# Loading the expert, down and output weights and the bias from SP's queue behind the first inputs, in a fused attention and expert layer

## The reference

```python
def attn(x, w_qkv, w_out):                       # 16 heads of 8
    q, k, v = split(x @ w_qkv)
    a = softmax(q @ k.T / sqrt(128))
    return (a @ v) @ w_out

def ffn(x, Wr, Wg, Wu, Wd, Sg, Su, Sd, bias):    # 8 experts, 2 taken, 1 shared
    top_v, top_i = top_k(x @ Wr + bias, 2)
    rw = zeros.at[top_i].set(softmax(top_v))
    h = silu(x @ Wg) * (x @ Wu)
    return sum_e(rw[e] * (h[e] @ Wd[e])) + silu(x @ Sg) * (x @ Su) @ Sd

x = x + layernorm(attn(layernorm(x)))
x = x + layernorm(ffn(layernorm(x)))
```

## Time and profile before

| | |
|---|---|
| median of 3 runs | 380.06 us (378.44 to 380.81) |
| span of the profiled execution | 378.7 us |
| PE busy | 359.4 us (95%) |
| DVE busy | 310.7 us (82%) |
| ACT busy | 267.4 us (71%) |
| POOL busy | 200.8 us (53%) |
| DMA, moved | 45.65 MB |

### The profile page before, as it was taken

The page is one execution under the profiler, slowest core; times in us unless marked ns, Lnnn a source line. Parts: engine busy times, 40 slices in busy tenths (PEclk is TensorE's granted clock), DMA queues, the critical chain, the costliest instruction groups (busy, mean ns, idle before and its releaser), DMA issues.

```text
span 378.7 us, 10110 instructions
## 1 busy us (share of the span) xinstructions
PE 359.4 (95%) x3342; PEld 231.8 (61%) x3342; DVE 310.7 (82%) x788; ACT 267.4 (71%) x511; POOL 200.8 (53%) x518
## 2 busy tenths in 40 slices
PE   7898799999999999999999999999999999999992
PEld 7866556455465557575657565665665566677872
DVE  8476579989899998989998889999998896767461
ACT  4563368788977877887878877786868876964522
POOL 5723121615556374848472835674744655858644
PEclk9999899999999999999999999999999999999998
DMA  2139766847534728557616937544773042222201
GB/s 76 44 105 150 180 123 131 183 140 153 148 105 137 181 54 205 142 144 174 140 58 165 230 103 182 132 121 121 161 181 113 7 115 74 85 74 69 71 8 38
DMA packets 59922, 45.65 MB, mean 121 GB/s; under 512 B 8966, under 2 KB 56966, under 8 KB 59870
## 3 DMA queue, kind: packets, MB, share of 16 engines
q1 hardware_dynamic: 56638, 44.02, 46.5%
q10 hardware_dynamic: 3232, 0.99, 2.3%
HBM read 26.69 MB, written 17.81 MB: 118 GB/s over the span
## 4 chain that ended last, share of the span: by engine, by line
PE 61%; issue 10%; POOL 7%; DMA 6%; DVE 6%; ACT 4%; SPq 3%; ACTq 1%; POOLq 0%; DVEq 0%
PE pvp L674 13%; PE sc L643 8%; PE sc L658 8%; PE bank_d L824 7%; PE bank_d L840 6%; PE bank_d L825 5%; PE bank_d L681 3%; PE bank_a L726 3%; DVE mx L1036 3%; DMA pv_dram<-pv_sb 2%; POOL rstd L1178 2%; POOL hidden L1245 2%; PE bank_d L797 2%; PE bank_a L735 2%; DMA ks<-qk_dram 1%
## 5 line engine op out<-in xcount | busy, mean ns | idle before, releaser
L1036 DVE TENSOR_REDUCE mx<-sc 128x4 f32<-128x1024 f32 x128 | 153.9, 1220 | 20.3 <-PE sc L643 19.4
L888 ACT ACTIVATE pr<-sc 128x1024 f32<-128x1024 f32 x128 | 129.8, 1024 | 32.8 <-PE sc L658 32.3
L674 PE MATMUL pvp<-pr,va 128*32 128x256 f32 x1024 | 68.5, 385 | 0.0
L824 PE MATMUL bank_d<-x3T,wg_sb 128*128 128x256 f32 x160 | 54.8, 424 | 1.3 <-DVE hidden L1134 1.2
L658 PE MATMUL sc<-qs,ks 51*128 51x256 bf16 x512 | 48.8, 274 | 4.1 <-DMA qs<-mT 2.0
L643 PE MATMUL sc<-ks,qs 48*128 48x256 bf16 x512 | 48.9, 274 | 1.1 <-DVE mx L1036 0.7
L1173 POOL TENSOR_TENSOR vareps<-mv,eps 128x2 f32<-128x2 f32 x64 | 12.6, 197 | 67.0 <-DVE mv L1028 67.0
L825 PE MATMUL bank_d<-x3T,wu_sb 128*128 128x256 f32 x160 | 47.6, 379 | 0.0
L1245 POOL TENSOR_TENSOR hidden<-hidden,rwb 128x256 f32<-128x256 f32 x60 | 43.0, 731 | 6.6 <-DMA rwb<-rw_dram 6.3
L1178 POOL TENSOR_TENSOR rstd<-vareps,mhalf 128x2 f32<-128x2 f32 x64 | 44.5, 696 | 0.0
L971 ACT ACTIVATE th<-bank_d 128x256 f32<-128x256 f32 x80 | 30.7, 384 | 18.4 <-PE bank_d L825 16.7
(11 more groups left out here) (113 smaller groups left out, 503.9 us busy)
## 6 DMA issues: line engine op xcount, KB each, us to landing
rwb<-rw_dram SPq DMA_DIRECT2D x30, 256.0 KB, 4.3
qk_dram<-parts SPq DMA_DIRECT2D x30, 192.0 KB, 3.4
qs<-qk_dram SPq DMA_DIRECT2D x30, 192.0 KB, 4.5
ks<-qk_dram SPq DMA_DIRECT2D x30, 192.0 KB, 5.1
qk_dram<-parts SPq DMA_DIRECT2D x30, 128.0 KB, 3.0
pv_dram<-pv_sb SPq DMA_DIRECT2D x14, 256.0 KB, 2.8
x_sb<-in_L_attn_x_dram SPq DMA_DIRECT2D x16, 128.0 KB, 3.0
out_dram<-x SPq DMA_DIRECT2D x16, 128.0 KB, 1.8
```

What stands on the lines that cost most here:

```text
L674: mm = pe.matmul(pvp[32 * j:32 * j + 32, g, :], values[:, X * c + 4 * g + j, 32 * tt:32 * tt + 32], pr[:, k, c * N:(c + 1) * N], start=(tt ...
L824: pe.matmul(bank_d[bank][:, 0:N], wg_sb[:, ORDER[n], :], x3T[b % 2][:], start=True, stop=True)
L888: nc.scalar.activation(pr[:, 2 * s:2 * s + 2, :].rearrange("p k n -> p (k n)"), sc[PAIR["s2", b, s]][:].rearrange("p u c n -> p (u c n)"), ...
L1036: nc.vector.tensor_reduce(mx[b % 2][:, :, :, s].rearrange("p c u -> p u c"), sc[PAIR["s1", b, s]][:], AX.X, ALU.max).then_inc(max_done, 1)
```

## The change

All four weight loads move. `load_wgu` and `load_wd` go from ACT's stream to SP's, and together with `load_wout` and `load_bias` they get ticks 60, 64, 66 and 68, between `load_x(1)` (48) and `load_x(2)` (72). The setup copies of `lay` and the zeroing of `rw`, which stood ahead of the tick loops on ACT and DVE, become steps at ticks 1 to 5, which leaves their place. `sel1` waits for the copies of its own part alone (4 at each later part, where it was 8 at the first), `v` gets a wait on `xT_copied`, and `fill` is called at `pv_n` and `selq`, for which the table has no entry.

```diff
 TIMES = {
+    "lay0a": [1], "lay0b": [2], "rwz": [3], "lay1": [4], "lay2": [5],
...
-    "load_wgu": [1289],
+    "load_wgu": [60],
...
-    "load_wd": [1677],
+    "load_wd": [64],
...
-    "load_wout": [2049],
+    "load_wout": [66],
...
-    "load_bias": [2209],
+    "load_bias": [68],
...
@@ SP
+            def load_wgu():
+                sp.dma_start(wr_sb[:], Wr).then_inc(wgu_load, DMA)
+                sp.dma_start(wg_sb[:, 4, :], Sg).then_inc(wgu_load, DMA)
+                sp.dma_start(wu_sb[:, 4, :], Su).then_inc(wgu_load, DMA)
+                for e2 in range(2):
+                    es = slice(4 * e2, 4 * e2 + 4)
+                    half = slice(F * e2, F * e2 + F)
+                    sp.dma_start(wg_sb[:, 0:4, half], Wg[es].rearrange("c d f -> d c f")).then_inc(wgu_load, DMA)
+                    sp.dma_start(wu_sb[:, 0:4, half], Wu[es].rearrange("c d f -> d c f")).then_inc(wgu_load, DMA)
...
             for tick in TICKS:
+                if due(tick, "load_wgu") == 0:
+                    load_wgu()
+                if due(tick, "load_wd") == 0:
+                    load_wd()
...
@@ PE
+                    pe.wait_ge(xT_copied, b + 1)
                     turn(a_empty)
...
                             pe.wait_ge(lay_done0, 6)
-                            pe.wait_ge(lay_done, 8)
+                        else:
+                            pe.wait_ge(lay_done, 4 * n)
...
@@ ACT
             for tick in TICKS:
-                if due(tick, "load_wgu") == 0:
-                    load_wgu()
-                if due(tick, "load_wd") == 0:
-                    load_wd()
+                for n in (1, 2):
+                    if due(tick, f"lay{n}") is not None:
+                        act.wait_ge(identb_done, 1)
+                        act.wait_ge(lay_zeroed, 1)
+                        for src, dst in lay_steps(n):
+                            nc.scalar.copy(dst, src).then_inc(lay_done, 1)
```

More of the change, by code:

```diff
@@ L536, in load_bias, with load_wd @@
                 sp.dma_start(bias_sb[:], src).then_inc(bias_load, DMA)
+            def load_wgu():
[7 more added lines that the diff above has]
+                    sp.dma_start(wu_sb[:, 0:4, half], Wu[es].rearrange("c d f -> d c f")).then_inc(wgu_load, DMA)
+            def load_wd():
+                sp.dma_start(wd_sb[:, 4, :], Sd).then_inc(wd_load, DMA)
+                for e2 in range(2):
+                    es = slice(4 * e2, 4 * e2 + 4)
+                    sp.dma_start(wd_sb[F * e2:F * e2 + F, 0:4, :], Wd[es].rearrange("c f d -> f c d")).then_inc(wd_load, DMA)
             load_x(0)
@@ L709, in _ @@
                     if (b := due(tick, f"pv_{n}")) is not None:
+                        fill(f"pv_{n}", b)
                         pv(b, n)
@@ L755, in _ @@
                 if due(tick, "selq") is not None:
+                    fill("selq", 0)
                     pe.wait_ge(kh_copied, 2)
@@ L854, in apply @@
                                          scale=rstd[L][b % 2][:, t:t + 1]).then_inc(applied[L], 1)
[L856 to L876, removed]
-            for tick in TICKS:
-                if due(tick, "load_wgu") == 0:
-                    load_wgu()
-                if due(tick, "load_wd") == 0:
-                    load_wd()
+            for tick in TICKS:
+                for n in (1, 2):
[4 more added lines that the diff above has]
+                            nc.scalar.copy(dst, src).then_inc(lay_done, 1)
                 for s in range(X):
@@ L995, in _ @@
             nc.vector.memset(lay_words[:, 0:X * WIDTH], 0.0).then_inc(lay_zeroed0, 1)
[L996 to L1001, removed]
             def permute_qk():
@@ L1030, in _ @@
             for tick in TICKS:
+                for n in range(2):
+                    if due(tick, f"lay0{'ab'[n]}") is not None:
+                        dve.wait_ge(identb_done, 1)
+                        dve.wait_ge(lay_zeroed0, 1)
+                        for src, dst in list(lay_steps(0))[3 * n:3 * n + 3]:
+                            nc.vector.tensor_copy(dst, src).then_inc(lay_done0, 1)
+                if due(tick, "rwz") is not None:
+                    for r in range(2):
+                        nc.vector.memset(rw[r][:, TT * E:], 0.0).then_inc(rw_zeroed, 1)
                 for s in range(X):
```

## The result

The changed kernel takes 383.17 us (median of 14 runs, 381.61 to 385.21), the kernel before took 379.62 us beside it (14 runs, 377.72 to 381.83). The ratio is 1.0119, with a 95% interval of 1.0099 to 1.0139: slower by 3.8 to 5.3 us by the ratio, 3.55 us by the medians. The forecast was +1.5 us. The sign of the sum was right and the time lies in the range, but the change is more than twice as large as forecast and, by the ratio, just beyond the bound of 1% at which I had put 0.21. The range was 7 us wide, so that the time lies in it says little for the sum. In what follows a comparison is of medians, with the ratio and its 95% interval beside it; one execution of `e8_sp_old_place` (383.69 us, 1.8% above the fastest of that kernel) is left out as a slow one.

A forecast was written before the change was run, and what follows sets the result against it. PE's own work sets the pace from 60 us on, so its entry there counts: +5.4 (late x) +0.9 (clock at start) -3.3 (stall, landing) -1.5 (clock at 42 us) = +1.5, giving 381.6 us; range 378.2 to 385.2.

The forecast's parts named there:

- the sum: Whole kernel: two losses and two gains in the first 60 us add up to +1.5 us; chance 0.53.
- the bound of 1%: Whole kernel: about 3.8 us, what a measurement can tell from no change; chance 0.21 of being slower by more.
- x of batch 2, the issues: SP's stream at the start: nineteen DMAs ahead take 11.9 us, so this x is issued at 14.1 us.
- x of batch 2, the landing: Start of the kernel: this x lands 2.4 us after its issue, at 16.5 us (14.5 to 18.4).
- D: Start of the kernel: delay of everything behind the late x of batch 2, 5.4 us, with ends at 3.4 and 7.3.
- The chain behind x: DVE, ACT and POOL steps of batch 0: POOL's `part3` begins 2.65 us after x lands, instead of at 13.70 us.
- The clock at the start: PE idle from about 14 to 18.5 us, then at a lower clock: +0.9 us, bounds 0 and 1.7.
- Stall and landing of the maxima: Before `s2_0` of batch 0: without ACT's stall, and with maxima landing faster, 3.3 us gained; 1.4 if landing stays slow.
- The clock at 42 us: PE from 42 to 46 us: without the waits ahead the clock stays up, 1.5 us gained, bounds 0 and 1.7.
- slower by over 1%: Rival, whole kernel: late transfers or a long clock drop at the start give +6.5 us, 386.6 us; chance 0.21.
- the even exchange: Rival, whole kernel: the two waits are exchanged one for one, -1.4 us, 378.7 us, no change; chance 0.2.
- SP was free at 47 us: SP, relieved of 5.3 us of issues there, sends batch 3's spill earlier, but nothing in PE's waits names it.

The follow-up runs named there:

- e8_sp_old_place: All four weight loads issued from SP, but at the ticks of the kernel before; 377.75 us against 378.34 for the kernel before, ratio 0.9989.
- e9_bias_behind: The changed kernel with only the bias load moved behind the x of batch 3; 380.50 us against 379.21 for the kernel before, ratio 1.0038.
- e10_bias_alone: The kernel before with only the bias load moved ahead of the x of batch 2; 378.65 us in one run, against 378.34.
- e7_before_look1: The kernel before, unchanged, profiled once more; 379.31 us.

## Why the prediction was right and wrong

**x of batch 2, the issues.** Right. 11.9 us were forecast for the nineteen, 11.5 measured; issue at 14.1 and 13.71 us. For the gate and up loads (held back by a full DMA system, less at the start) the real price was the lower bound; the two of `Wd` cost nearly their old price, 1.39 against 1.53 us.

**x of batch 2, the landing.** This is the step that failed most, in size and not in kind: the sum gives x 2.4 us from issue to landing, and it took 4.0. With it D, forecast as 5.4 us, was 6.7. It lands at 17.75 instead of 16.5, inside the stated 14.5 to 18.4. The step took the landing time from loads with no other DMA ahead; the bias ahead of it adds 1.4 to 1.9 us, which `e9_bias_behind` and `e10_bias_alone` show apart. The trace of the kernel before has 3.8 us for the bias's own landing, more than the 2.7 to 3.0 of x loads sixteen times its size. The prediction doesn't ask what that does to the DMA behind it.

**The chain behind x.** Right. D = landing - 11.05 gives 6.7 us; POOL's `part3` starts at 20.48 instead of 13.70, 6.8 us late. Nothing had slack.

**The clock at the start.** Right in kind (the low clock is there from 17 to 24 us, behind 6 us of idle PE), a little high in size: 0.9 forecast, `s1_0` 7.3 and 6.8 us late in the two profiles, so 0.1 to 0.6 beyond D. PE's idle time was longer than forecast, too: until 19.9 us, not 18.5.

**Stall and landing of the maxima.** Right against the execution that I used: 3.3 us forecast, 7.30 - (45.56 - 41.63) = 3.4 measured. Against `e7_before_look1`, with its shorter wait, it is 2.6.

**The clock at 42 us.** Right against the execution that I used (1.5 us forecast, 16.46 - 15.00 = 1.5 measured), and the second failure against the medians. The sum books a low clock as the profiled execution had it, behind `s2_0`. Of three other executions with the same start none has it there in full, and their mean gain behind `s2_0`, with that of the profiled one, is 0.75 us. Its neighbour, the long wait for `mT`, was also at its largest in that execution. I took the bounds of the term as 0 and 1.7 us, but then added 1.4 us to get from span to median, as if this execution were a median one.

The terms, with the mean of the four executions of the old start and of the two of the changed kernel in the last column:

| term of the sum, us | forecast | measured up to `osel` |
|---|---|---|
| x of batch 2 (D) | +5.4 | +6.7 |
| clock at the start | +0.9 | +0.35 |
| stall and landing of the maxima | -3.3 | -3.0 |
| clock at 42 us | -1.5 | -0.75 |
| sum | +1.5 | +3.3 |

So of the 2.05 us that the forecast lacks by the medians, 1.3 is the later landing, 0.75 the clock at 42 us and 0.3 the stall, less 0.55 for the clock at the start. The landing is shown by two experiments; the other differences rest on six traces. What is left, 0.25 us by the medians and more by the ratio (3.8 to 5.3 us slower), stays open: the two profiled executions of the changed kernel took 381.91 and 382.28 us, about 1 us under its median, so no trace shows a median run of it. The chances went wrong with the same steps: a D of 7.3 was in my text as the condition for slower by over 1%, together with "one more term" going wrong, and nearly that happened. The range's lower end is also 0.5 us off by its own words, since the even exchange is worked out as 378.7 and the range starts at 378.2. The span of the changed profile, 380.1, agrees with the sum's 380.2 only by luck: the sum against the prediction's own execution is +2.5 us at `osel` (60.56 against 58.09), and behind `osel` that trace happens to be 1.1 us shorter than the old one.

That `sel1`'s waits, `v`'s new wait and the moved setup copies cost nothing is borne out: `sel1` starts at 12.37 us, before it was 12.39. That SP was free at 47 us brought nothing that a trace shows.

## What to carry to other kernels

Price a DMA that moves ahead of others by what it takes of its queue's issuing engine and by what it does to the landing of the next one, not by its bytes: here 72 KB in nine DMAs made x land 7.1 us later, of which their transfer would be 0.4. Then take off the slack that the waiting engine has: the ten DMAs with 0.94 MB took SP nearly as long to issue (5.6 us, the nine 5.9), and 4.6 us of slack hid all but 0.8 of their delay. Put weights that are needed late behind the last input that is needed early; with the large weights ahead of that input or behind it and the small pieces late, the move gained 2.6 to 3.3 us where it had lost 3.55. And before a gain is booked for a wait or a low clock seen in one profile, look at the clock and time of the other runs and take a second profile: the same low clock cost 1.5 us behind the last wait and 0.3 ahead of it, and in which place it falls differs between executions of one kernel.

## What the runs showed of the hardware that I had not expected

- A broadcast of 32-byte rows to 128 partitions (8 KB) makes a 128 KB load directly behind it on the same queue land after 4.2 to 4.3 us instead of 2.7 to 3.0, at an otherwise quiet start (`e10_bias_alone`); behind `w_out` it was 4.0 against 2.1 (changed kernel and `e9_bias_behind`).
- `w_out`'s pieces of 8 KB (16 rows of 512 bytes) keep SP for 0.66 to 0.68 us each with the gaps (5.46 us for eight at 8 us, 5.30 at 47 us), longer than a 128 KB load of 512 runs of 256 bytes (0.44 to 0.51).
- The same seven loads took ACT 5.7 us at 28 us and SP 3.5 us at 2 us; issued by SP at 28.8 us, beside the stacking of q and k, they took 4.2, the last of them 1.16. So on one engine the same issues took longer when other transfers were under way.
- Three executions of one kernel were granted three different clocks at 38 to 46 us: 0.50 from 42 us on, 0.50 from 38 us on, and 1.00 throughout. In `e10_bias_alone` 0.50 from 38 to 40 us made `s2_0` at most 0.3 us later (41.12 us, against 40.84 without a low clock), because PE had a wait there to lose.
